# A wait on the landing of the previous row group, put behind the first gather of each row group

## The reference

```
x = layernorm(x + gru(segment_sum(x[src] @ W_msg.T + b_msg + edge_embed[type], dst), x))
h = x
for layer in 0, 1, 2:                    # ei adds a self loop for every node
    ee  = ea @ enc_w + enc_b             # edge attributes, 16 wide
    m   = h[ei[1]] + ee                  # layers 1 and 2 concatenate instead of adding
    agg = segment_sum(m, ei[0])          # 212500 rows into 12500 nodes
    h   = relu(bn(agg @ w1 + b1)) @ w2 + b2     # and a relu between layers
out = layernorm(x + h)
```

## Time and profile before

| what | value |
|---|---|
| median of 3 runs | 7267.47 us (7256.35 to 7285.77) |
| the profiled execution | 7257.37 us |
| its span, first to last instruction | 7255.4 us |
| busy PE, PEld, DVE, ACT, POOL over the span | 75%, 47%, 52%, 46%, 58% |
| the layers | about 4030 to 7214 us of the span |

### The profile page before, as it was taken

How to read it: one execution, slowest core, us unless ns; L and a number is a source line. 1 busy time by engine, 2 the same in 40 slices (tenths; PEclk the granted TensorE clock), 3 DMA queues, 4 the chain that set the end, 5 groups by cost and what they waited for, 6 DMA issues and landing times.

```text
span 7255.4 us, 87916 instructions
## 1 busy us (share of the span) xinstructions
PE 5459.2 (75%) x26247; PEld 3380.7 (47%) x26429; DVE 3769.8 (52%) x14165; ACT 3309.0 (46%) x4432; POOL 4197.9 (58%) x4243
## 2 busy tenths in 40 slices
PE   3376666666666663566668799999898999899998
PEld 1133333333333331333334566666666666666666
DVE  6566667676666663455557444444333333343443
ACT  1154545454545452122213466666555555455554
POOL 5555545455545555666660566666666666676665
PEclk9988888887888886677666899999999999999999
DMA  6255545455555553333331666666665666666665
GB/s 226 57 127 123 123 121 129 116 128 123 129 120 123 128 140 98 87 100 100 98 101 54 191 195 174 185 188 188 214 182 168 191 188 191 209 186 172 179 180 147
DMA packets 1068177, 1066.40 MB, mean 147 GB/s; under 512 B 494051, under 2 KB 784501, under 8 KB 1067701
## 3 DMA queue, kind: packets, MB, share of 16 engines
q1 hardware_dynamic: 889573, 782.05, 38.2%
q0 software_dynamic: 178128, 278.65, 15.2%
HBM read 747.21 MB, written 216.68 MB: 133 GB/s over the span
## 4 chain that ended last, share of the span: by engine, by line
PE 49%; another core or an unknown queue 19%; DVE 15%; issue 8%; ACT 8%; DMA 1%; SPq 1%; POOL 0%; ACTq 0%; DVEq 0%; POOLq 0%
PE ps L2939 26%; PE ps L2724 5%; PE ps L2909 4%; ACT MTB L2435 3%; DVE BIG L2011 2%; ACT MT L2431 2%; PE ps L2822 2%; PE ps L2873 2%; DVE BIG L1953 2%; PE ps L2783 1%; DVE BIG L2173 1%; DVE BIG L2005 1%; PE ps L2707 1%; DVE BIG L2042 1%
## 5 line engine op out<-in xcount | busy, mean ns | idle before, releaser
L3021 POOL DMA_INDIRECT GL<-h_gathered,IDXA x2058 | 2104.2, 1022 | 1292.2 <-issue 561.2
L2939 PE MATMUL ps<-MSR,HP 128*128 128x512 f32 (+1 forms) x9000 | 2390.8, 412 | 149.5 <-issue 76.1
L2988 POOL DMA_INDIRECT rec_q<-BIG x1563 | 1506.3, 964 | 1377.2 <-DVE BIG L2030 523.9
L2549 ACT CAST MSR<-MS 128x1024 fp32r<-128x1024 uint8 (+1 forms) x1500 | 1489.4, 1028 | 1304.8 <-PE ps L2939 901.6
L2939 PEld LDWEIGHTS ps<-MSR,HP 128*128 128x128 f32 x9000 | 1689.6, 196 | 596.3 <-issue 167.3
L2724 PE MATMUL ps<-MTB,XPS 128*128 128x512 bf16 x4228 | 1304.1, 424 | 159.1 <-ACT MTB L2435 96.6
L2233 DVE CAST MSR<-MS 128x1024 fp32r<-128x1024 uint8 (+1 forms) x750 | 522.9, 701 | 1235.4 <-PE ps L2939 780.5
L2431 ACT CAST MT<-ps 128x512 uint16<-128x512 f32 x735 | 428.0, 582 | 1203.5 <-remote 863.7
L2435 ACT CAST MTB<-MT 128x1024 bf16<-128x1024 uint8 x735 | 767.9, 1045 | 55.3 <-remote 8.4
L3003 POOL DMA_INDIRECT BIG<-x_parts,SRCq x611 | 582.6, 954 | 346.4 <-issue 160.6
L2707 PE MATMUL ps<-BIG 128*128 128x256 bf16 x1470 | 427.9, 291 | 378.8 <-ACT MT L2431 290.0
(11 more groups left out here) (238 smaller groups left out, 5657.1 us busy)
## 6 DMA issues: line engine op xcount, KB each, us to landing
MS<-counts SPq DMA_DIRECT2D x1080, 256.0 KB
counts<-BIG SPq DMA_DIRECT2D x360, 256.0 KB
XPS<-x_parts SPq DMA_DIRECT2D x192, 384.0 KB
GL<-h_gathered,IDXA POOLq DMA_INDIRECT x2058
rec_q<-BIG POOLq DMA_INDIRECT x1563
rec_q<-BIG SPq DMA_DIRECT2D x44, 490.0 KB, 10.5
HTI<-h_cols SPq DMA_DIRECT2D x72, 256.0 KB
h_dense<-PCL SPq DMA_DIRECT2D x30, 512.0 KB
```

The lines of the kernel that those rows point to most:

```text
L2549: s.copy(MSR[:, g % RM, :, 0:w].rearrange("p t (c s) -> p t c s", s=P), MSB[:, i % MR, 0:4 * w].rearrange("p (c h s t) -> p h t c s", h=2, ...
L2939: got = t.matmul(bank[:, 0:w], HP[:, d, part, :], MSR[:, g % RM, d % 2, 0:w], start=d + part == 0, stop=lay > 0 and d + part == BD, skip_g ...
L2988: g.indirect_dma_start(out=RAd, out_offset=bass.IndirectOffsetOnAxis(ap=POSI[:, c:c + 1], axis=0), in_=RECA[q % 3][:, c - a, :], in_offset ...
L3021: g.indirect_dma_start(out=GL[:, r % LR, i, 0:3 * P], out_offset=None, in_=HGd[lay], in_offset=bass.IndirectOffsetOnAxis(ap=IDXA[:, a + i: ...
```

## The change

POOL gets one more wait in the layers. Behind the first gather of a row group and in front of its second, it waits until all gathers of the row group in front have landed. The very first row group of all has no such wait.

```
                         if r >= LR:
                             g.wait_ge(row_sum.sem, r - LR + 1)
                         for i in range(TS[r % 2]):
+                            if r and i == 1:
+                                g.wait_ge(rows_in[(r - 1) % LR].sem, layer_rows(r - 1))
                             g.indirect_dma_start(
                                 out=GL[:, r % LR, i, 0:3 * P], out_offset=None, in_=HGd[lay],
                                 in_offset=bass.IndirectOffsetOnAxis(ap=IDXA[:, a + i:a + i + 1], axis=0)).then_inc(*rows_in[r % LR].inc(16))
```

## The result

The changed kernel takes 7627.03 us (median of 4 runs, 7622.73 to 7632.19) against 7263.74 us (median of 4, 7256.35 to 7285.77): 1.049 times as long, 95% interval 1.0474 to 1.0506. That is 363 us slower, where 126 were forecast. The direction was right, the size was not, and the time lies above the range.

What follows compares the result with a forecast made beforehand. The PE was taken to bound the layers, with POOL running ahead. Waits of 2.0 us less 1.57 us free, x 294 pairs, gave 126 us on 7257 to 7267, so 7385 us; range 7240 to 7545.

Steps and rivals of the forecast that it cites:

- POOL's slack of 463 us: In the layers: 3184 us less 2721 us of back-to-back gathers leaves POOL 463 us, 1.57 us a pair of row groups.
- the first 463 us cost nothing: POOL's first 463 us of new waiting are free, because it waits there instead of behind the full ring.
- the ring gone as cover: Six row groups of gathered rows in front; once POOL falls behind, every late landing shows at the PE.
- the PE waiting at L2909: PE row matmuls in the layers get about 100 us of idle time in front of them, in place of 16.
- the landing time: Time until a gather's rows are in, counted from q0 packets: 2.1 to 2.3, 3.1 to 3.4 and 4.8 to 5.2 us.
- 2.0 us a pair: Waits before second gathers: 0.6 us behind a group of four plus 1.4 behind a three, against 1.57 us free.
- The wake-up of 0.27 us: Time from a met condition to POOL's gather start, taken from its wait on the PE; bounds 0 and 0.6 us.
- the first case: The 949th gather, last of a group of four: landing at most 2.3 us, plus 0.27 under 2.64, so no wait.
- Three chosen instants: Landings read at the 949th, 315th and 707th gathers, where POOL pauses: condition met in time, 0.9 and 2.8 us late.
- Hidden: Rival: landings come sooner with fewer gathers in flight, waits stay under 1.57 us a pair; 7257 to 7267 us; chance 0.24.
- Faster: Rival: gathers kept off the count tile and HP loads let ACT and DVE widen sooner; 7225 us; chance 0.12.
- A larger bill: Rival: landings stay long because of SP's loads, about 2.6 us a pair, 300 us slower, 7557 us; chance 0.15.

Runs made afterwards that it cites:

- e1: Changed kernel with the wait on the row group two in front instead of one: 5877.46 us, ratio 0.9993 to the kernel before.
- e11: Changed kernel with only three gathers in each row group from the seventh on, wait values lowered to match: 6247.42 us, ratio 1.0638 to the kernel before.
- e9: The changed kernel run again, unaltered, on the chips of the experiments: 6598.97 us, ratio 1.1243 to the kernel before.
- e12: Changed kernel with the wait only in the first five row groups behind the first one of each layer: 5867.92 us, ratio 0.9994 to the kernel before.
- e8: Changed kernel with count tile loads bringing only their first half from the sixth on: 6466.72 us, ratio 1.0993 to the kernel before.
- e3: Changed kernel with the wait in front of the first gather of a row group instead of the second: 7603.46 us, ratio 1.2929 to the kernel before.
- e6: Changed kernel with every gather reading by its block's first index column: 6443.08 us, ratio 1.0958 to the kernel before.

## Why the prediction was right or wrong

**The frame held.** POOL's slack of 463 us, the count of 587 waits, "the first 463 us cost nothing", the ring gone as cover and the PE waiting at L2909: the profile after shows each. L2909's idle time was forecast at about 100 us and became 553; POOL's waits at 500 to 600 us and became 893. e1 and e11 show the mechanism from both sides, and e9 shows the subtraction of the slack on a chip where it is 105 us.

**The step that failed is the landing time, and with it the term "2.0 us a pair".** That term was the price of the two waits, 0.6 us behind a group of four and 1.4 behind a group of three. By the gaps in front of the second gathers of the changed kernel they are 1.36 and 1.66 us, 3.0 a pair; with POOL's busy time 44 us lower, 0.15 us a pair, 2.85. (2.85 - 1.57) x 294 = 376 us against the 374 us by which the span grew. The parts:

- *The wake-up of 0.27 us was right.* It was taken from POOL's wait on the PE. Behind a full DMA semaphore it is 0.26 us (6008.76 to 6009.02 above).
- *The landing was read too short, because started packets were counted.* "The landing time has no row of its own, but it can be counted" took the start of a gather's last packet for its landing. The condition waits for the semaphore. By the mean waits (wait + 2.64 - 0.26) the landing in the changed kernel is 3.74 us behind a group of four and 4.04 behind a group of three, and the same count of packets over all gathers of that trace gives 3.10 and 3.35: 0.6 and 0.7 us too little, 1.3 us a pair. The forecast stood at 2.97 and 3.77, which is 0.3 us above that count in the sum, and so 1.0 us a pair was missing. The semaphore updates that are left in the trace of before say the same of the three gathers that were read: the last ones that it holds come 2.63, 3.65 and 5.55 us behind the starts, so the landings are at least that long, where the count had at most 2.3, 3.4 and 5.2. So in the first case, too, the condition would not have been met: 2.63 + 0.27 is over 2.64.
- *Three chosen instants and a weight by eye* did less harm. Counted over all gathers of the trace of before, the last packet starts on average 3.18 us behind the last gather of a four and 3.84 behind that of a three. By the forecast's own rule that is 0.81 + 1.47 = 2.28 us a pair, 209 us in all: still little more than half of what was measured.

That 3.77 for a group of three lies near the 4.04 is partly luck: it stands above the 3.35 of the count, and this made up for part of what the count leaves out.

**Sizing against slack.** Only the excess over 463 us counts, so an error of 1.0 us in 2.0 became one of three times in the result. The excess is 294 x (price - 1.57), so each 0.1 us of price is 29 us of time, and a range for the price would have given the range for the time.

**The rivals.** *Hidden* needed a mean landing below 3.16 us; it is 3.74 and 4.04. *Faster*: e12 took the place where it was strongest and found nothing, and in the changed kernel the dense matmuls' idle time did fall, from 149.5 to 26.9 us, while the PE now stands before L2909 for 553.4 us, so no time was gained. *A larger bill* (300 us) came nearest, and its landings were right: 3.6 to 3.9 us behind a four and 4 to 4.5 behind a three. Its own sum was wrong. Those landings with a wake-up of 0.27 make 2.9 to 3.7 us a pair and not 2.6, which is 380 us or more and not 300. Its reason, SP's loads, is shown for 134 of the 893 us of waits (e8) and for the rest it is a correlation in e9.

**Against the page.** The estimate of 2.2 us from the Trainium skill (DMA: Bandwidth & Descriptors, Anatomy of one DMA — SWDGE (gpsimd) path) seemed to agree with the earlier trace rows, but only as long as packets were counted. To the full semaphore the shortest gather of e3 takes 2.5 us and the median one 3.2, so the measured times are longer than the estimate even at their shortest.

## What to carry to other kernels

A wait that is put on an engine with slack is priced as (sum of all waits) minus (slack), and an error in the first comes through whole in the second: write down both, and the excess as their difference. Take the landing time of a DMA from its semaphore, by the chain or by a wait that it ends, and not from the packets that have started; take it at instants that are drawn evenly, not where the engine happens to pause. Slack belongs to the machine as much as to the kernel: the same waits cost 363 us on one chip and 728 on another.

## What the runs showed of the hardware that was not expected

- The same program took 7264 us on the first chip and 5870 to 5881 on the others. Most of it lies in front of the layers (4030 against 2986 us). The cause was not tried.
- POOL starts a gather 0.26 to 0.27 us after what it waits for, be it a matmul or the full semaphore of a DMA. The start of that DMA's last packet lies another 0.31 to 0.56 us before, in the wait shown at 6004.98.
- Where two conditions stand in front of one gather and the landing comes last, the start comes 0.74 us after the landing in place of 0.26 (e3).
- The landings of equal gathers spread widely: the chain of e3 has one of 2.57 us, and the longest in that trace is 7.4 us.
- A gather of 128 rows by the seventh index column lands about 0.6 us later than one by the first, at equal bytes: 1.61 against 1.03 us of waiting (e9, e6).
- A met condition in front of an indirect DMA adds nothing to the 0.30 us between two of them (e1).
